# Layer norm of the projection blocks cut into pieces and moved one block earlier, with GpSimd's first work held back

## The reference

```
x = x + attention(layernorm(x))        16 heads of 16 channels, softmax over all 2048 keys
x = x + ffn(layernorm(x))              token shift, sigmoid gate, squared relu
layernorm(x) = (x - mean) / sqrt(var + 1e-5)
q, k, v = layernorm(x) @ W.T + b
```

## Time and profile before

| what | value |
|---|---|
| median of three runs | 2793.02 us |
| the profiled execution | 2794.98 us |
| its span, first to last instruction | 2792.6 us |
| mean granted TensorE clock | 0.998 |
| TensorE busy | 2743.2 us, 98% |
| VectorE busy | 2506.8 us, 90% |
| ScalarE busy | 2490.0 us, 89% |
| GpSimd busy | 374.3 us, 13% |
| projection stage, about | first 237 us |
| mix stage, about | last 230 us |

### The profile page before, as it was taken

One profiled execution on the slowest core, in us unless ns is written; L12 is line 12 of the kernel. 1 busy time (PEld: TensorE's weight loads), 2 busy tenths in 40 slices (PEclk: granted clock), 3 DMA queues, 4 the chain that ended last, 5 costly groups with the idle time before them and its releaser, 6 DMA issues.

```text
span 2792.6 us, 60098 instructions
## 1 busy us (share of the span) xinstructions
PE 2743.2 (98%) x23676; PEld 930.3 (33%) x23676; DVE 2506.8 (90%) x4853; ACT 2490.0 (89%) x2863; POOL 374.3 (13%) x751
## 2 busy tenths in 40 slices
PE   8999999999999999999999999999999999999999
PEld 5543222222222222222222222222222222224776
DVE  6567999999999999999999999999999999985774
ACT  6668999999999999999999999999999999997555
POOL 6662000000000000000000000000000000103451
PEclk9999999999999999999999999999999999999999
DMA  5552000000000000101010101010001100212531
GB/s 169 179 165 86 22 22 22 22 22 22 22 22 22 19 25 13 31 8 32 12 33 11 33 11 33 11 33 12 27 18 31 33 21 22 59 39 80 164 127 46
DMA packets 135290, 124.36 MB, mean 45 GB/s; under 512 B 49888, under 2 KB 117344, under 8 KB 135008
## 3 DMA queue, kind: packets, MB, share of 16 engines
q1 hardware_dynamic: 135008, 120.52, 14.1%
HBM read 72.75 MB, written 47.19 MB: 43 GB/s over the span
## 4 chain that ended last, share of the span: by engine, by line
PE 77%; SPq 10%; DVE 4%; ACT 4%; DMA 2%; issue 2%; POOL 0%; ACTq 0%
PE psum L1331 32%; PE psum L1234 16%; PE psum L1290 15%; SPq L153 4%; SPq L158 3%; PE psum L1359 2%; PE psum L1766 2%; SPq L126 2%; PE psum L1249 2%; PE psum L447 2%; SPq L127 2%; DMA a_qs<-q_parts 2%; PE psum L1372 2%; PE psum L1754 2%; ACT m_gate L954 1%
## 5 line engine op out<-in xcount | busy, mean ns | idle before, releaser
L1040 DVE TENSOR_REDUCE a_mx<-psum 128x1 f32<-128x512 f32 x3096 | 1945.8, 683 | 98.4 <-PE psum L1290 77.7
L1234 PE MATMUL psum<-a_qs,a_ks 50*128 50x512 f16 x4096 | 791.7, 383 | 10.2 <-ACT p_x L954 0.5
L1290 PE MATMUL psum<-a_ks,a_qs 48*128 48x512 f16 x3596 | 695.1, 383 | 20.1 <-DVE a_mx L1040 10.8
L954 ACT ACTIVATE m_gate<-psum 128x1024 f32<-128x1024 f32 x684 | 674.3, 1033 | 37.3 <-PE psum L1234 34.6
L954 ACT ACTIVATE m_y<-psum 128x1024 f32<-128x1024 f32 x682 | 672.3, 1033 | 37.4 <-PE psum L1234 34.5
L954 ACT ACTIVATE p_x<-psum 128x1024 f32<-128x1024 f32 x682 | 672.3, 1033 | 37.3 <-PE psum L1234 34.5
L1331 PE MATMUL psum<-m_gate,a_vst 128*32 128x256 f32 (+1 forms) x4568 | 413.0, 433 | 0.8
L1331 PE MATMUL psum<-p_x,a_vst 128*32 128x256 f32 (+1 forms) x4568 | 412.0, 432 | 0.8
L1331 PE MATMUL psum<-m_y,a_vst 128*32 128x256 f32 (+1 forms) x4552 | 411.8, 433 | 0.8
L1234 PEld LDWEIGHTS psum<-a_qs,a_ks 50*128 50x128 f16 x4096 | 198.8, 93 | 604.6 <-ACT p_x L954 135.6
L1035 DVE CUSTOM_DVE_ANT_0 a_copied<-psum,a_copied 128x512 f32<-128x512 f32 x500 | 323.5, 684 | 22.1 <-PE psum L1290 22.0
(11 more groups left out here) (142 smaller groups left out, 1662.0 us busy)
## 6 DMA issues: line engine op xcount, KB each, us to landing
m_x<-x SPq DMA_DIRECT2D x24, 512.0 KB, 5.5
a_qs<-q_parts SPq DMA_DIRECT2D x384, 32.0 KB, 2.1
sums<-a_o SPq DMA_DIRECT2D x256, 34.0 KB
q_parts<-m_split SPq DMA_DIRECT2D x16, 512.0 KB, 3.4
v_rows<-m_v SPq DMA_DIRECT2D x16, 512.0 KB, 2.7
k_parts<-m_split SPq DMA_DIRECT2D x16, 512.0 KB, 3.9
a_ks<-k_parts SPq DMA_DIRECT2D x64, 128.0 KB
a_vin<-v_rows SPq DMA_DIRECT2D x64, 128.0 KB, 5.6
```

Source lines behind the costliest of these rows:

```text
L954: ac.activation(p_sb[n % WEIGHTS][:, 2 * pair:2 * pair + 2, :], psum[:, at:at + 2, :], ACT.Exp, scale=SCALE).then_inc(s_exp, 1)
L1040: dve.tensor_reduce(peak, psum[:, bank(at), :], AX.X, ALU.max).then_inc(s_mx, 1)
L1234: mm = te.matmul(psum[:, pair_of_banks(u) + par, :], ks[row:row + MR, (it // QB) % 2, pair, c * P:(c + 1) * P], qs[row:row + MR, it % QRIN ...
L1290: te.matmul(psum[:, bank(slot(n, par)), :], qs[row:row + SR, pit % QRING, at:at + P], keys, start=True, stop=True).then_inc(s_sp, 1)
```

## The change

- The layer norm chain gets a second buffer (`works[pair % 2]`), so that it can run while the values of the pair before are still being read.
- In the stage's opening, the whole chain of pair 1 and the normalising of block 2 stand before the loop (they were its first items).
- In the loop, for the even block blk: half of `statistics(blk + 4)` stands behind pack 0 and half behind pack 1, half of `statistics(blk + 5)` behind pack 3 and half behind pack 4, all of block blk. In block blk + 1 the aggregates stand behind pack 0, seed and first Newton step behind pack 1, the second behind pack 2, the third and the offset behind pack 3.
- SyncE's program is not changed.
- GpSimd waits, before the low parts of block 0, until VectorE has normalised block 2.
- Block 0 takes the same order as the others on TensorE and ScalarE (`turned(1)` before the second half of v).
- In the mix stage the last inverse stands before `residual(4)`, no longer behind it.

```diff
+    works = [ahead.work] + [sb("p_work1", [P, 6, 2 * TT], F32)]
...
         pool.memset(mx[:, 1, 1:G * TT:2, KB - 1:KB], LEAST).then_inc(s_one, 1)
+        alone.wait(pool, 0, f"third{TT - 1}")
         for blk in range(BLOCKS):
             lesser_parts(blk, blk % 2)
...
-            if blk == 0:
-                keep_v(blk, 1)
-                keep_turned(blk + 1)
-                continue
...
-        def statistics(blk):
+        def statistics(blk, half=None):
 
             dve.wait_ge(s_x[blk % 4], DMA * (blk // 4 + 1))
-            for t in range(TT):
+            for t in range(TT) if half is None else range(2 * half, 2 * half + 2):
...
+        def seed(pair):
+            ve, half, y = work_of(pair)[:3]
             ln.wait(dve, pair, f"meanvar{2 * TT - 1}")
+            if pair == 2:
+                alone.wait(dve, 0, f"second{TT - 1}")
+            elif pair > 2:
+                an.wait(dve, 2 * pair - 3, f"norm{TT - 1}")
...
-            if pair == 1:
-                alone.wait(dve, 0, f"second{TT - 1}")
-            elif pair:
-                an.wait(dve, 2 * pair - 1, f"norm{TT - 1}")
...
         statistics(2)
         statistics(3)
+        whole_norm(1)
+        normalised(2)
         for blk in range(0, BLOCKS, 2):
+            pair, more = blk // 2 + 2, blk + 4 < BLOCKS
             lead(blk, 0)
-            if blk + 2 < BLOCKS:
-                means(blk // 2 + 1)
-                newton(blk // 2 + 1)
-            if blk == 0:
-                normalised(2)
-            for at in range(1, 5):
-                lead(blk, at)
+            if more:
+                statistics(blk + 4, 0)
+            lead(blk, 1)
+            if more:
+                statistics(blk + 4, 1)
+            lead(blk, 2)
+            lead(blk, 3)
+            if more:
+                statistics(blk + 5, 0)
+            lead(blk, 4)
+            if more:
+                statistics(blk + 5, 1)
             lead(blk + 1, 0)
-            if blk + 4 < BLOCKS:
-                statistics(blk + 4)
+            if more:
+                means(pair)
             lead(blk + 1, 1)
-            if blk + 4 < BLOCKS:
-                statistics(blk + 5)
-            for at in range(2, 5):
-                lead(blk + 1, at)
+            if more:
+                seed(pair)
+                newton(pair, 0)
+            lead(blk + 1, 2)
+            if more:
+                newton(pair, 1)
+            lead(blk + 1, 3)
+            if more:
+                newton(pair, 2)
+                offsets(pair)
+            lead(blk + 1, 4)
...
             gated(blk)
-            if blk + 4 < BLOCKS:
-                residual(blk + 4)
             if blk == 0:
                 for n in range(inputs.SLICES):
                     inputs.invert(dve, B - 1, n)
+            if blk + 4 < BLOCKS:
+                residual(blk + 4)
```

More of the change, by code:

```diff
@@ L536, in stage_attend @@
     kd_parts = [sb(f"p_kd{s}", [P, KH, PARTS, TB // 2], F16) for s in range(2)]
-    stats, mv, work = ahead.stats, ahead.mv, ahead.work
+    stats, mv = ahead.stats, ahead.mv
+    works = [ahead.work] + [sb("p_work1", [P, 6, 2 * TT], F32)]
     s_w = {n: sem(f"p_s_w{n}") for n in "qkvb"}
@@ L892, in normalise @@
                 at = blk % 2 * TT + t
+                work = works[blk // 2 % 2]
                 an.done(ac.activation(xn[blk % 2][:, t, :], x_sb[blk % 4][:, t, :], ACT.Identity,
@@ L990, in scalar @@
                 copy(0)
-            if blk + 2 < BLOCKS:
+            if 0 < blk < BLOCKS - 2:
                 normalise(blk + 2, 0)
             keep_v(blk, 1)
-            if blk + 2 < BLOCKS:
+            if 0 < blk < BLOCKS - 2:
                 normalise(blk + 2, 1)
@@ L1082, in gains, with work_of @@
             dve.tensor_tensor(scaled[:, :], bias[:, :], gain[:, :], ALU.mult).then_inc(s_gain, 1)
-        ve, half, y, y_squared, z, offset = (work[:, n, :] for n in range(6))
+        def work_of(pair):
+            return [works[pair % 2][:, n, :] for n in range(6)]
         def first_alone():
@@ L1120, in normalised @@
         def normalised(blk):
+            y, offset = work_of(blk // 2)[2], work_of(blk // 2)[5]
             ln.wait(dve, blk // 2, "offset")
@@ L1143, in means, with newton, offsets, whole_norm @@
             ln.wait(dve, pair, "shift")
-            if pair == 1:
-                alone.wait(dve, 0, f"second{TT - 1}")
-            elif pair:
-                an.wait(dve, 2 * pair - 1, f"norm{TT - 1}")
             ln.done(dve.tensor_scalar(y.bitcast(I32), half.bitcast(I32), -1.0, RSQRT_SEED, ALU.mult, ALU.add))
[L1150 to L1162, removed]
+        def newton(pair, n):
+            ve, _, y, y_squared, z, _ = work_of(pair)
+            ln.wait(dve, pair, f"newton{n - 1}c" if n else "seed")
+            ln.done(dve.tensor_tensor(y_squared, y, y, ALU.mult))
+            ln.wait(dve, pair, f"newton{n}a")
+            ln.done(dve.scalar_tensor_tensor(out=z, in0=y_squared, scalar=-0.5, in1=ve, op0=ALU.mult,
+                                             op1=ALU.mult))
+            ln.wait(dve, pair, f"newton{n}b")
+            ln.done(dve.scalar_tensor_tensor(out=y, in0=z, scalar=1.5, in1=y, op0=ALU.add, op1=ALU.mult))
+        def offsets(pair):
+            y, offset = work_of(pair)[2], work_of(pair)[5]
+            ln.wait(dve, pair, "newton2c")
             ln.done(dve.scalar_tensor_tensor(out=offset, in0=mv[:, :, 0], scalar=-1.0, in1=y, op0=ALU.mult,
                                              op1=ALU.mult))
+        def whole_norm(pair):
+            means(pair)
+            seed(pair)
+            for n in range(3):
+                newton(pair, n)
+            offsets(pair)
         def lead(blk, n):
@@ L1179, in vector @@
         statistics(1)
-        means(0)
-        newton(0)
+        whole_norm(0)
         normalised(1)
@@ L1453, in tensor @@
             lead(blk, 3)
[L1454 to L1457, removed]
             if blk + 1 < BLOCKS:
```

## The result

The changed kernel takes 2825.93 us, the median of four runs (2824.63 to 2828.22), against 2793.07 us for the kernel before on the same chip: ratio 1.0118, 95% interval 1.0101 to 1.0136. That is 32.9 us slower. The profiled execution took 2828.22 us (span 2825.8); between the two profiled executions the difference is 33.2 us. The prediction was 2821, range 2808 to 2833.

The account below looks back on a forecast made before the run. TensorE was taken to bound the kernel, holding 77% of the chain that ended last. Terms +30.7 + 0 - 1.6 + 0 - 1.0 = +28.1 on the profiled 2794.98 us gave 2823.1, or 2821 against the median; range 2808 to 2833.

Parts of the forecast that it names:

- The odd blocks: Blocks 7, 9, 11: pack 0 waits 7.7 us for statistics of late-loaded x(blk+5), plus 2.6 us clock each; +30.7 us total.
- Even blocks 8 and 10: Pack 2 waits 1.4 us for statistics of x(blk+4), in place of 1.56 us; 0, bounds -1 and +1 each.
- Block 12: Projection stage: no more statistics there, so its 1.56 us wait before a pack goes; -1.6 us.
- the inverse: Mix stage: its 1.8 us now run while VectorE is idle, ahead of a 1.49 us TensorE wait; -1.0 us.
- The opening and block 6: Block 6 starts 3 us sooner, then loses it waiting 6.5 us at pack 1; net 0, bounds -4 and +4.
- the opening and block 6 cost more: Rival, 0.10: GpSimd's queue pushes block 3's store, key loads and x(9) by 4 us; +36, 2829, at worst 2836.
- faster: Rival, 0.05: early statistics do not hold the packs and winnings in blocks 6 to 12, opening and inverse stand; -15, 2778.

Follow-up runs that it names:

- the odd statistics later: Changed kernel with only the statistics of x(blk+5) put later, behind packs 0 and 1 of block blk+1, chain pieces behind packs 2 to 4; 2795.78 us, ratio 1.0010.
- the sooner loads: Changed kernel with each load of x issued a block sooner in SyncE's program, ahead of the stores; 2778.17 us, ratio 0.9944.
- without the hold: Changed kernel without GpSimd's wait for VectorE to normalise block 2; 2825.34 us, ratio 1.0113.
- the hold alone: Kernel before, with only GpSimd's wait until block 2 is normalised added; 2793.85 us, ratio 0.9999.
- the statistics put back: Changed kernel with both statistics where they stood before, the chain in pieces between packs of the pair's own even block; 2786.59 us, ratio 0.9979.
- the hold to the offset: Changed kernel with loads of x a block sooner and GpSimd held only until the chain of pair 1 has ended; 2778.33 us, ratio 0.9946.
- the inverse alone: Kernel before, with only the last inverse moved ahead of residual(4) in the mix stage; 2792.96 us, ratio 0.9998.

## Why the prediction was right, and which terms were mis-sized

**The odd blocks (+30.7 forecast, +30.4 measured).** This was the step that decided, and it held in each link. The statistics of x(11) were to start at T + 8.2 (they did at T + 8.35), TensorE was to be freed at T + 9.6 (T + 9.75), and to wait 7.7 us; the three waits are 7.77, 7.99 and 7.43, in sum 23.2 for 23.1. The clock was to cost 2.6 us each; what the three blocks took beyond 13.76 us and their waits is 3.14, 2.05 and 2.19, in sum 7.4 for 7.8. The experiment with the odd statistics later gives these 30 us back, and the one with the sooner loads names the cause. The estimate of 3.2 us for a 512 KB transfer, from the Trainium skill's page "DMA: Bandwidth & Descriptors", section "Anatomy of one DMA — SWDGE (gpsimd) path", is not what SyncE's queue shows: issue to statistic took 6.0 us again.

**Even blocks 8 and 10 (0 forecast, bounds -1 and +1 each; -0.5 and +2.1 measured).** The new waits were to be 1.4 us in place of 1.56; they are 1.04 and 1.98. The term for block 10 was mis-sized, and by the clock: of its +2.06 the longer wait is 0.42, and 1.5 is the first half of v behind it, 3.50 us where it takes 1.99 in blocks 7 to 9; the pack behind that has the last 0.1. It was no accident of one profile: block 10 took 17.72 us without the hold and 17.52 with the odd statistics later. The granted clock there, TensorE alone:

```profile
185.70:189.20 3.50, 3.50 (x12) 0.55 0.00 0
```

I had clock loss behind the long waits only, since the 1.56 us of before never showed it.

**Block 12 (-1.6)** and **the inverse (-1.0, bounds 0 and -1.5).** Block 12 gave -1.62. The inverse's wait is gone in the trace: the projection follows the product by 3.46 us in place of 5.10. But from the start of block 13 to the end of the span the changed kernel took 2596.0 us against 2596.2, so 0.2 us in all: the lag grew by 0.95 us ahead of that place and by 0.5 behind it, and I did not follow why. The -1.0 is seen in the wait and not in the time. VectorE's eight instructions now stand at 2611.05, behind 3.06 us of idle time that a DMA ended:

```profile
2611.05 1.83 DVE L291 RECIPROCAL m_inv<-m_den 128x32 f32<-128x32 f32 x8 [3.06 <-DMA m_den<-sums]
```

**The opening and block 6 (0 forecast, bounds -4 and +4; +3.1 measured).** The step at fault is block 5, which I had at 11.44 us. The opening itself went as worked out: block 1 at 25.67 (24.6 forecast, the stage having started 1.2 us later), block 2 at 37.11 (36.0), the normalising done at 28.9 (27.9). Blocks 2, 3 and 4 gave back 0.9, 1.0 and 0.6 us, less than the 2.0, 1.1 and 1.0 forecast. But block 5 took 15.95 us. GpSimd, started late, was still at full work, and that made the chain of pair 3 late in two ways. It began late: the load of x(7) stands behind the key difference store of block 2, which GpSimd's queue held until 62.04, and its statistic came at 66.58, where the kernel without the hold has it at 63.00. And it ran beside GpSimd. From SyncE's timeline of after the load, from VectorE's the statistic and the chain's first instruction, and from ScalarE's the wait for its last (76.08 to 76.33):

```profile
62.45 0.51 SPq L684 DMA_DIRECT2D m_x<-x  x1
```

```profile
66.58 1.41 DVE L1133 BATCH_NORM_STATS2 m_stats<-m_x 128x6 f32<-128x256 f32 x4 [10.78 <-DMA m_x<-x]
...
68.81 0.51 DVE L1148 TENSOR_SCALAR p_work<-m_mv 128x8 f32<-128x8 f32 x1
```

```profile
76.37 1.09 ACT L896 ACTIVATE m_xn<-m_x,p_work 128x256 f32<-128x256 f32 x2 [3.08 <-DVE p_work L1169]
```

The chain took 7.5 us and kept ScalarE waiting 3.08; behind that its copies of the projections were late, TensorE waited 2.78 us and then ran its k projections at the lower clock (5.33 us for eight against 3.71 in block 5 of before). Either remedy was enough to end it: with the loads sooner the chain was done at 60.6, and without the hold at 69.3, and block 5 took 11.44 us in both. I had followed GpSimd's backlog to ScalarE's waits for stores, and not to VectorE's small instructions nor to the load of x(7), on which ScalarE hangs as well. 1.2 of the +3.1 us is no work of the change: block 0 started that much later in this profile. From there block 6 went as forecast in its length, a wait of 6.01 us (6.5) and 22.0 us in all (22.8), but from 89.87 and not 86. That it came so near is luck in part: the chain of pair 4 ended at 101.06 and not at 97.8, and the block's own late start made up for it.

**The rival "the opening and block 6 cost more"** is thus the true mechanism in part, with another middle: not the store of block 3 that pushes the key loads and x(9), but the store of block 2 that pushes x(7), and with it the chain of pair 3 that pushes ScalarE. **The rival "faster"** named its own condition, x(blk + 5) loaded some 5 us sooner, ahead of the v store, and its price, -15 us and 2778. With that condition made by hand the kernel takes 2778.17. The condition did not hold in the change. The sum of winnings was right, but its terms made up for each other: by the two profiles block 6 gave 5.0 us (6.3 in the sum), the stage up to block 6 4.7 (3), blocks 7 to 12 5.1 (4.8).

**The whole sum.** Forecast +28.1, measured +33.2 in the profiled executions: odd blocks -0.3 against the forecast, blocks 8 and 10 +1.5, the stretch up to block 7 +3.1, and the inverse +0.8. The misses nearly all have one sign and are small beside the odd blocks' 30.

**Best version.** The changed kernel with the sooner loads, 2778.2 us, beats both. What keeps its block 6 at 14.74 us is ScalarE, which waits for a late key difference store:

```profile
88.47 0.78 ACT L944 ACTIVATE m_whole<-psum,p_sb,p_gain 128x512 f32<-128x512 f32 x1 [2.15 <-DMA k_difference_parts<-p_kd]
```

## What to carry to other kernels

Work moved ahead in one engine's queue moves its wait ahead too, and everything behind it on that engine then waits for the transfer: before an instruction is moved a block sooner, find where the load that it needs is issued, and what stands before that load. Move the load by the same step or leave both. And a gain ahead of a later wait counts for nothing until that wait is gone, so two edits that are each worth nothing or less alone can be worth 15 us together.

## What the runs showed of the hardware that was not expected

- **The length of a short wait alone does not tell the clock behind it.** In block 5 TensorE waited 2.77 or 2.78 us before the same k projections in four kernels. In the changed one the eight behind it took 5.33 us at a granted clock of 0.68; with the hold alone, the statistics put back and the odd statistics later they took 3.70 or 3.71 us at 1.00, and block 5 took 14.3 us and not 15.95. Waits of 1.98 us (changed kernel, block 10) and 2.12 us (odd statistics later, block 10) were followed by a granted clock of 0.55 to 0.65; a wait of 2.12 us in block 9 of the kernel with the statistics put back was followed by 1.00. TensorE alone, 2 us behind each of the two waits of 2.12 us, the odd statistics later first:

```profile
163.10:165.10 2.00, 2.00 (x8) 0.65 0.00 0
```

```profile
143.10:145.10 2.00, 2.00 (x14) 1.00 0.90 283
```

- **A small VectorE instruction beside GpSimd waits for a whole GpSimd instruction.** VectorE's and GpSimd's timelines in block 6 of after:

```profile
94.88 1.12 DVE L1148 TENSOR_SCALAR m_work<-m_mv 128x8 f32<-128x8 f32 x1
96.03 0.17 DVE L1150 TENSOR_SCALAR m_work<-m_work 128x8 int32<-128x8 int32 x1
96.24 1.00 DVE L1152 TENSOR_SCALAR m_work<-m_work 128x8 int32<-128x8 int32 x1
97.28 1.07 DVE L1158 TENSOR_TENSOR m_work<-m_work 128x8 f32<-128x8 f32 x1
98.39 1.07 DVE L1160 SCALAR_TENSOR_TENSOR m_work<-m_work 128x8 f32<-128x8 f32 x1
99.49 0.17 DVE L1163 SCALAR_TENSOR_TENSOR m_work<-m_work 128x8 f32<-128x8 f32 x1
```

```profile
92.47 3.50 POOL L120 MEMSET a_ks<- 32x4096 f16 x1
96.05 3.39 POOL L839 TENSOR_TENSOR m_split<-m_whole,m_split 128x512 f16<-128x512 f32 x3
```

The four that took 1.00 us or more end near 96.0, 97.2, 98.4 and 99.5: where the fill and each of GpSimd's three instructions (3.39 for three, 1.13 each) end. The one that starts as GpSimd stops takes 0.17 us, as do the ones behind it. The Trainium skill, page "SBUF — State Buffer", section "SBUF: two separate sides", states that the two engines share a pair of ports as an exclusive lock, held for the whole instruction, and that on VectorE's side it concerns instructions in a two-port mode or with two inputs in SBUF. The profile does not show the mode. By that rule one instruction costs VectorE up to a GpSimd instruction however small it is, and this trace agrees: 1.0 to 1.1 us for 0.17. The kernel with the hold to the offset shows it at its largest: a shift on 128x8 (L1151) that began at 35.37 together with a fill of 3.50 us took 3.53 us. The statistics did not feel GpSimd: four took 1.41 us at 76.48, beside it, and 1.40 at 15.24, with it held. In a chain of 13 it came to 6.2 us for pair 4 in block 6 and 7.5 for pair 3 in blocks 4 and 5, against 2.6 in the opening (17.46 to 20.06), where GpSimd was held.
- **The stage's start varies.** Block 0 began between 12.7 and 14.2 us in the profiled executions; the changed kernel's 14.15 against 12.96 accounts for 1.2 of the 3.1 us that block 7 starts later, and the change has no work there.
- **So does block 6 for the same code.** In the kernel of the inverse alone, whose projection stage is that of before, blocks 1 and 6 took 15.05 and 18.61 us where the earlier trace rows have 16.40 and 19.72. A difference of 1 or 2 us in one block of two profiles says nothing; waits that repeat from block to block do.
